# Five routed blocks moved between the heads of the matrix memory, one bank for its query products, result gathers behind all masks

## What is computed

```python
# cross attention (per sequence, 8 heads of 16 features)
log_D = log_fg_mat + ig[:, None, :]
max_log_D = jnp.max(log_D, axis=-1, keepdims=True)
D_mat = jnp.exp(log_D - max_log_D)
qk = jnp.einsum('hsd,htd->hst', qh, kh) / np.sqrt(DH)
C = qk * D_mat
normalizer = jnp.maximum(jnp.abs(C.sum(axis=-1, keepdims=True)), jnp.exp(-max_log_D))
h = jnp.einsum('hst,htd->hsd', C / (normalizer + EPS), vh)

# mixture of experts: 8 experts, 128 -> 512 -> 128, two per token
h = jax.nn.gelu(jnp.einsum('bsd,edi->bsei', x, ew1) + eb1)
all_outputs = jnp.einsum('bsei,eid->bsed', h, ew2) + eb2
moe_out = jnp.einsum('bse,bsed->bsd', weights_E, all_outputs)
return x + _mlp(x, sh_w1, sh_b1, sh_w2, sh_b2) + moe_out
```

## Time and profile before

| | |
|---|---|
| median of 3 runs | 2514.45 us (2510.74 to 2525.26) |
| the profiled execution | 2516.93 us |
| its span, first to last instruction | 2514.5 us |
| mean granted clock of TensorE | 0.896 of full |
| busy: PE, DVE, ACT, POOL | 1936.6, 1697.9, 1113.0, 842.5 us |

### The profile page before, as it was taken

One profiled execution on the slowest core, in us unless ns is written; L12 is line 12 of the kernel. 1 busy time (PEld: TensorE's weight loads), 2 busy tenths in 40 slices (PEclk: granted clock), 3 DMA queues, 4 the chain that ended last, 5 costly groups with the idle time before them and its releaser, 6 DMA issues.

```text
span 2514.5 us, 41889 instructions
## 1 busy us (share of the span) xinstructions
PE 1936.6 (77%) x14136; PEld 1372.4 (55%) x14136; DVE 1697.9 (68%) x3985; ACT 1113.0 (44%) x3168; POOL 842.5 (34%) x775
## 2 busy tenths in 40 slices
PE   2785697778886898678876788679876888675698
PEld 1454366645673457545674467445664567454355
DVE  8985893679656893769556993769556883723355
ACT  2462365335642465236542565236632565232234
POOL 0551562217420651227321651236321651211000
PEclk8997899889997999889987999789987999787799
DMA  4000012101030013101030103001120103042000
GB/s 134 1 1 9 15 54 71 63 10 60 5 121 11 22 47 99 35 11 59 18 107 11 52 17 110 24 13 58 39 86 11 66 2 113 13 169 90 9 13 21
DMA packets 72770, 117.33 MB, mean 47 GB/s; under 512 B 7823, under 2 KB 46871, under 8 KB 72039
## 3 DMA queue, kind: packets, MB, share of 16 engines
q1 hardware_dynamic: 67014, 101.42, 12.3%
q0 software_dynamic: 5536, 13.12, 1.7%
HBM read 95.18 MB, written 18.81 MB: 45 GB/s over the span
## 4 chain that ended last, share of the span: by engine, by line
DVE 37%; PE 36%; issue 14%; POOL 6%; ACT 5%; DMA 1%; SPq 1%; DVEq 0%; POOLq 0%; ACTq 0%
PE bank L1336 34%; DVE work L495 11%; DVE bank L504 5%; DVE work L513 3%; DVE work L493 3%; DVE max L782 2%; ACT work L941 2%; POOL hid L1244 1%; PE bank L1340 1%; DVE acc L698 1%; POOL work L1212 1%; POOL work L1224 1%; ACT hid L941 1%; PE bank L1481 1%; DVE negmax L515 1%
## 5 line engine op out<-in xcount | busy, mean ns | idle before, releaser
L1336 PEld LDWEIGHTS bank<-work 128*128 128x128 f32 (+2 forms) x5152 | 372.3, 187 | 171.1 <-issue 143.8
L1336 PE MATMUL bank<-work 128*128 128x128 f32 (+2 forms) x5152 | 403.0, 293 | 55.7 <-DVE max L782 29.2
L941 ACT ACTIVATE work<-bank 128x512 f32<-128x512 f32 (+1 forms) x560 | 246.5, 518 | 283.6 <-PE bank L1336 257.5
L495 DVE TENSOR_TENSOR work<-bank,table_space 64x512 f32<-64x512 f32 x512 | 352.1, 688 | 6.8
L1212 POOL TENSOR_TENSOR work<-work 128x512 f32<-128x512 f32 x128 | 163.3, 1276 | 385.7 <-DVE work L495 284.6
L941 ACT ACTIVATE work<-work 128x512 f32<-128x512 f32 (+1 forms) x338 | 196.7, 618 | 170.1 <-DVE work L576 84.8
L941 ACT ACTIVATE work<-work,negmax 128x128 f32<-128x128 f32 x512 | 199.1, 390 | 100.3 <-DVE negmax L515 100.3
L1219 POOL TENSOR_TENSOR work<-sb_ident,nrm 128x512 f32<-128x512 f32 x128 | 133.0, 1039 | 284.2 <-ACT nrm L941 284.2
L1336 PE MATMUL bank<-work,table_space 128*128 128x512 f32 x256 | 140.5, 630 | 90.0 <-DVE negmax L515 59.5
L941 ACT ACTIVATE hid<-bank,w_ring 128x128 f32<-128x128 f32 x480 | 136.1, 370 | 163.6 <-PE bank L1336 163.5
L493 DVE TENSOR_TENSOR work<-bank,table_space 128x512 f32<-128x512 f32 x256 | 174.0, 679 | 48.7 <-PE bank L1336 22.6
(11 more groups left out here) (287 smaller groups left out, 3478.6 us busy)
## 6 DMA issues: line engine op xcount, KB each, us to landing
w_ring<-in_w_routed SPq DMA_DIRECT2D x120, 514.0 KB, 4.3
x_quad<-x_sorted SPq DMA_DIRECT2D x24, 256.0 KB, 2.8
y_sorted<-y_quad SPq DMA_DIRECT2D x24, 256.0 KB, 2.5
x_T<-in_x_T POOLq DMA_DIRECT2D x9, 256.0 KB, 3.1
x_row<-in_x_row POOLq DMA_DIRECT2D x9, 256.0 KB, 4.5
ctx_T<-in_ctx_T SPq DMA_DIRECT2D x8, 256.0 KB, 2.7
work<-in_ctx_row SPq DMA_DIRECT2D x8, 256.0 KB, 2.9
out<-act_row SPq DMA_DIRECT2D x8, 256.0 KB, 2.3
```

What stands on the lines that cost most here:

```text
L495: last = v.tensor_tensor(rows(wk[i + 1][o]), rows(src[p]), sinT[o, s].unsqueeze(1).broadcast_to([DH0, GB, N]), ALU.mult)
L941: return nc.scalar.activation(o, i, f, **k)
L1336: return nc.tensor.matmul(o, l, r, start=start, stop=stop, skip_group_check=True)
```

## The change

Five edits, all between the end of the gate computation and the combination:

1. With heads beside them, units 12 to 16 (blocks 10 to 14) and the down product of block 9 are no longer computed ahead of `xattn` but between its heads, by two tables on PE (`UP_AT`, `DOWN_AT`), one on ACT (`GELU_AT`) and places in DVE's loop.
2. All query products go through bank 7, so the product of head s waits for the mix of head s - 1, and it stands behind the value product of head s - 2. Maxima alternate between banks 0 and 5, value products are in banks 1 and 2.
3. The masked contexts have four tiles of their own, so POOL no longer waits for the transposed rows ahead of masks 2 and 3.
4. POOL makes all 8 masks first; then it waits for the stores, then computes the context mean (`cbc`, before on DVE in `attn1`), then gathers 8 times in a row.
5. The transposes of the last routed rows stand at unit 10 instead of unit 12.

The pieces of the diff are, in this order: the tables; `xattn` of VectorE; `xattn` of ScalarE; `rows_back` and `xattn` of GpSimd; `xattn` of TensorE.

```diff
+        head_ctx, decay1, mix1 = wk[16:20], wk[14:16], wk[12:14]
+        nv_bank, max_bank = (1, 2), (0, 5)
...
+        BEFORE_X = 12
+        UP_AT, DOWN_AT = {0: 12, 1: 13, 3: 14, 4: 15, 5: 16}, {0: 11, 3: 12, 4: 13, 5: 14, 6: 15, 8: 16}
+        GELU_AT = {1: (12, 13), 3: (14, 15), 5: (16,)}
...
@@ -573,21 +579,25 @@
                         last.then_inc(arg_done, 1)
+                    if d and 4 <= s < 8:
+                        take_block(s + 6, g)
                     h = s - 1
                     if h >= 0:
...
+                    if d and s == 0:
+                        take_block(9, g)
+                if d:
+                    take_block(14, g)
                 dve.wait_ge(num, n1(H1))
...
@@ -1045,13 +1053,17 @@
+                gates_total(g, d)
                 for h in range(H1):
                     act.wait_ge(arg_done, tally(g, d, H1, h + 1))
+                    fn(decay1[h % 2], decay1[h % 2], ACT.Exp).then_inc(dmat, 1)
+                    if d and h in GELU_AT:
+                        for j in GELU_AT[h]:
+                            gelus(j, g, j == GELU_AT[h][-1])
...
@@ -1238,6 +1248,10 @@
                 for s in range(2):
                     pool.wait_ge(y_stored[s], g * (LOAD // 2 * 16) + LOAD // 2 * 16)
+                q.tensor_tensor(cbc[:], csum[:].unsqueeze(2).broadcast_to([128, GB, N]),
+                                per_token.unsqueeze(2).broadcast_to([128, GB, N]), ALU.mult).then_inc(ctx_mean, 1)
+                for i in range(TOPK * GB):
+                    gather(g, i)
@@ -1249,18 +1263,13 @@
-                    if d and 2 <= h < 4:
-                        pool.wait_ge(quad_tr, g * LOAD + h + 1)
-                    if d and h == 4:
-                        rows_back(g)
                     if h >= 4:
                         pool.wait_ge(qk1, tally(g, d, H1, h - 3))
...
-                    if d and 4 <= h:
-                        gather(g, 2 * h - 8)
-                        gather(g, 2 * h - 7)
+                if d:
+                    rows_back(g)
@@ -1593,38 +1601,46 @@
-                        mm(bank[4 + s % 2][:], sel24[:, s], m_parts[:]).then_inc(mx_bc, 1)
-                        pe.wait_ge(ctx_masked, n1(s + 1))
-                        if s == 0 and d:
-                            pe.wait_ge(y_out, g * BLOCKS + BLOCKS)
-                        if s >= 2:
-                            pe.wait_ge(c_done, n1(s - 1))
...
+                        mm(bank[max_bank[s % 2]][:], sel24[:, s], m_parts[:]).then_inc(mx_bc, 1)
+                    if d and s in DOWN_AT:
+                        experts_down(DOWN_AT[s], g, d, True)
+                    if d and s in UP_AT:
+                        experts_up(UP_AT[s], g, d, True)
                     h = s - 2
                     if h >= 0:
                         pe.wait_ge(c_done, n1(h + 1))
...
+                    if s < H1:
+                        pe.wait_ge(ctx_masked, n1(s + 1))
+                        if s == 0:
+                            pe.wait_ge(gate_eM, tally(g, d, 1, 1))
+                        else:
+                            pe.wait_ge(c_done, n1(s))
+                        for b in range(GB):
+                            last = mm(rows(bank[7])[:, b], rows(head_ctx[s % 4])[:, b], rows(seq_T)[:, b],
+                                      start=b == 0)
+                        last.then_inc(qk1, 1)
```

More of the change, by code:

```diff
@@ L91, in decoder @@
         rank = cols[:, 32:40]
+        per_token = cols[:, 20:20 + GB]
         block_no = cols[0:1, 72:72 + BLOCKS]
@@ L133, in decoder @@
         y_back = [hid[2], hid[3]]
-        head_ctx = [wk[2], wk[3]] + [x[:].rearrange("p b d -> p (b d)") for x in x_quad]
+        head_ctx, decay1, mix1 = wk[16:20], wk[14:16], wk[12:14]
+        nv_bank, max_bank = (1, 2), (0, 5)
         class Norm:
@@ L575, in xattn @@
                         for b in range(GB):
-                            last = v.scalar_tensor_tensor(rows(wk[s % 2])[:, b], rows(bank[4 + s % 2])[:, b],
+                            last = v.scalar_tensor_tensor(rows(decay1[s % 2])[:, b], rows(bank[max_bank[s % 2]])[:, b],
                                                           aT[:, b, s:s + 1], mask_ji[:], ALU.add, ALU.add)
                         last.then_inc(arg_done, 1)
+                    if d and 4 <= s < 8:
+                        take_block(s + 6, g)
                     h = s - 1
@@ L746, in heads_and_experts @@
                     take_block(7, g)
+                    take_rows(3, g)
                     take_block(8, g)
-                    take_block(9, g)
-                    take_rows(3, g)
-                    for i in range(10, BLOCKS):
-                        take_block(i, g)
+                    if not heads:
+                        for i in range(9, BLOCKS):
+                            take_block(i, g)
             def experts_norm(g):
@@ L1097, in heads_and_experts @@
                 if experts:
-                    for j in range(7, UNITS):
-                        gelus(j, g, j == UNITS - 1)
-                if heads:
-                    gates_total(g, d)
+                    for j in range(7, BEFORE_X if heads else UNITS):
+                        gelus(j, g, j in (BEFORE_X - 1 if heads else UNITS - 1,))
             def router_exp(g, d):
@@ L1319, in _ @@
             rows_back(G - 1)
-            for i in range(TOPK * GB):
-                gather(G - 1, i)
             attn1(G - 1)
@@ L1507, in unit @@
                         experts_down(j - 1, g, d, heads)
-                    if experts and j in (0, 4, 8, 12):
-                        rows_T(j // 4, g, d, heads)
+                    if experts and j in (0, 4, 8, 10):
+                        rows_T((j + 2) // 4, g, d, heads)
                 for s in range(H0 + 7):
@@ L1560, in heads_and_experts @@
                     gate_tot_columns(g, d)
-                for j in range(12, UNITS + 1):
-                    unit(j)
+                else:
+                    for j in range(BEFORE_X, UNITS + 1):
+                        unit(j)
             gw = res["gate_w"]
@@ L1595, in gate_tot_columns @@
                 pe.wait_ge(gate_tot, tally(g, d, 1, 1))
-                gate_columns(bank[0], gate[3], gate_T)
+                gate_columns(bank[7], gate[3], gate_T)
             def xattn(g, d):
                 n1 = lambda k: tally(g, d, H1, k)
-                nv = [bank[2 + i][:, 0:2 * H1 * (DH1 + 1)].rearrange("p (b h d) -> p b h d", b=2, h=H1)
-                      for i in range(2)]
+                nv = [bank[i][:, 0:2 * H1 * (DH1 + 1)].rearrange("p (b h d) -> p b h d", b=2, h=H1) for i in nv_bank]
                 for s in range(H1 + 2):
@@ L1608, in xattn @@
                             pe.wait_ge(gate_max, tally(g, d, 1, 1))
-                        mm(bank[4 + s % 2][:], sel24[:, s], m_parts[:]).then_inc(mx_bc, 1)
-                        pe.wait_ge(ctx_masked, n1(s + 1))
-                        if s == 0 and d:
-                            pe.wait_ge(y_out, g * BLOCKS + BLOCKS)
-                        if s >= 2:
-                            pe.wait_ge(c_done, n1(s - 1))
-                        for b in range(GB):
-                            last = mm(rows(bank[6 + s % 2])[:, b], rows(head_ctx[s % 4])[:, b], rows(seq_T)[:, b],
-                                      start=b == 0)
-                        last.then_inc(qk1, 1)
+                        if s == 1 and d:
+                            pe.wait_ge(quad_T, g * LOAD + LOAD)
+                        mm(bank[max_bank[s % 2]][:], sel24[:, s], m_parts[:]).then_inc(mx_bc, 1)
[3 more added lines that the diff above has]
+                        experts_up(UP_AT[s], g, d, True)
                     h = s - 2
@@ L1874, in layouts @@
     cols[:, 32:40] = 8 - np.arange(8)
+    cols[:, 20:20 + GB] = 1 / N
     cols[:, 72:] = np.arange(BLOCKS)
```

16 lines of the change are left out of this document (7 added, 9 removed).

## The result

The changed kernel takes **2624.73 us** (median of 4 runs, 2612.95 to 2628.7), the kernel before in the same job 2512.59. The ratio is **1.0434 [1.0403, 1.0466]**: 4.3% slower, 112 us. I had forecast 2585 (+70.5), in a range from 2558 to 2622: the measured time lies 2.7 above its end. The profiled execution takes 2623.85, its span is 2622.1, and TensorE's mean granted clock is 0.878 (before 0.896). Busy are PE 1989.7, DVE 1674.1, ACT 1166.9 and POOL 850.8 us. In the lines, argument, mix, copy, denominators and combination of DVE are now L582, L593, L700, L602 and L708; PE's products are L1343.

The account below looks back on a forecast made before the run. PE was taken to bound both merged stretches. Seven turns +60.9, group 0 +8.4 and last group +1.2 give +70.5 on the profiled 2516.93: 2587.4; that execution lies 2.5 above the median, so 2585 us, range 2558 to 2622 (80%).

Parts of the forecast that it names:

- The sign and the mechanism: Slower, 94%: in xattn, one bank makes a 3.18 us loop per head, copies behind the argument 5.40 in heads 4 and 5.
- both terms: Per turn: gate columns to denominators +5.2 us, denominators to combination +4.5.
- my sum: Whole kernel: seven turns +60.9, first group +8.4, last group +1.2, together +70.5 us.
- that rival: Merged stretch: TensorE falls to half clock; with half the heads there, some 8 us a turn, 2640 us; 9%.
- Group 0: Eight heads without blocks, half clock in the first two loops: +8.4 us; 6 if the clock rises at once, 15 if never.
- This is the largest term, and gathers set it, not PE: Behind the last copy: store wait, mean and 8 gathers start the combination at 1335.6, 9.7 us later than before.
- my rival: DVE's norms beside the gathers hold them up, at most 5 us: 2600 to 2620; 12%, shared with ACT's thin covers failing.
- ACT's loads: Three added pairs of table loads, 7.7 us a turn, costed at nothing because covered, by 0.2 and 0.1 us at the thinnest.
- the mean taken off DVE: In attn1, DVE loses the context mean; it waited there for PE's products anyway, so nothing gained.
- the combination shortened: Combination beside POOL's residual sums: 3.4 us instead of 4.40, so -1.0 a turn, bounds 0 and -2.1.
- "Unchanged": Behind the combination, attn1 was to stay unchanged; combination to the next gate columns was forecast at 0.

Follow-up runs that it names:

- PE kept busy: The changed kernel with products that nobody reads added where PE waits, no wait shortened: 2578.84 us, ratio 1.0249.
- the version in pairs: The kernel before with its gathers later but in pairs, a mask or half of the context mean on POOL between two pairs: 2504.94 us, ratio 0.995.

## Why the prediction was right, and where it was short

- **The sign and the mechanism were right.** One bank closes the loop at 3.26 a head, and the copy behind the argument makes it 5.54. Undoing the one saves 42 us, the other 55; both together leave 0.4% of the 4.3%. The size was short: +112 against +70.5. That the time came as near to the range as 2.7 is in part luck: the rest of the turns gave back 18.3 that no term of mine had.
- **The step that failed is the clock.** I costed every product of the merged stretch at its duration at full clock, and gave its fall 9%. It fell in all seven turns (0.75 to 0.87 against 1.00). That is 13.6 a turn where I had 5.2. With the waits filled the clock stays up and both terms are those of my sum, which shows the cause for the turns. I argued against the fall from `attn1`, where PE was busy 5.27 of 12.70 at 0.90; a nearer row was the earlier trace rows, where the query product of group 0 took 1.91 already. The Trainium skill (page "TensorE: Matmul & The Clock Gate", section "HAM oscillation — how this bites in real kernels") describes a loop whose waits let the clock fall on every pass. The rows here agree in part: the waits were 1.0 to 1.5 us, shorter than that loop's, and the clock fell behind some of them only (it held at 1.00 for 15.8 us in the turn shown). My price for that rival, 2640 with half the heads at half clock, was near.
- **Group 0 was the same mistake.** I let the clock rise after two loops (+8.4, "15 if it stays at half"). It stayed at 0.50: +17.1.
- **"This is the largest term, and gathers set it, not PE" was half right.** The gathers do end last (DVE waits 4.56 for a DMA). But they start behind PE's last blocks, and most of the delay is PE's: the denominators came 13.6 later, the gathers added 2.9 beyond the norms. At full clock, with PE kept busy, it was 5.8 and 4.5, near my 5.2 and 4.5.
- **The norms hold up the gathers a little.** In the turn shown, the gathers beside the norm's two products on DVE took 1.06 and 1.40 instead of 0.96; in the other six turns one took 1.06 to 1.08. The Trainium skill (page "SBUF — State Buffer", section "SBUF: two separate sides") names such a lock; here it would be worth 0.5 us in one turn and 0.1 in the others, against the 15 to 35 us in all of my rival.
- **ACT's loads and the mean taken off DVE changed nothing**, as costed; the combination shortened by 1.3 (forecast 1.0). The mean ahead of the gathers does cost: with three quarters of it ahead of the wait for the stores the combination started 13.3 to 13.5 behind the denominators, and not 13.4 to 14.2.
- **"Unchanged" for the rest of the turn was wrong**: it was 18.3 shorter over six turns. The granted clock goes with it. In the kernel before the rest takes 232.4 to 238.7 from turn to turn; these are two of its turns, then one of the changed kernel:

```profile
1047.43:1286.12 238.69, 193.75 (x1447) 132.87 (x1447) 167.10 (x370) 116.59 (x349) 89.27 (x80) 0.91 0.14 44
1330.36:1563.10 232.74, 187.62 (x1446) 129.68 (x1446) 167.12 (x369) 116.35 (x349) 89.34 (x80) 0.94 0.14 45
1688.33:1921.48 233.15, 187.90 (x1449) 129.96 (x1449) 165.99 (x369) 117.34 (x350) 90.29 (x81) 0.94 0.14 45
```

The work is the same, PE's time is 6 us longer where the clock is lower, and so is the turn. The clock is 0.91 in two of the six turns before, 0.93 in three and 0.94 in one; in the changed kernel it is 0.93 in one and 0.94 in five. At 0.94 the rest takes 232.7 before and 230.0 to 233.3 in the changed kernel; that the mean taken off DVE in `attn1` shortens it is not shown. What sets the clock there no run here isolates. Most of the 0.5% that the version in pairs gains lies there too: its combination starts only 0.4 earlier in a turn, and its rest takes 232.5 to 232.9 in four of six turns.

## What to carry to other kernels

Before work is put into an engine's gaps, ask what it waits for there: a product placed behind a wait, or a copy queued behind another operation on the reader's engine, turns the gap into a longer loop. If the engine is TensorE, price every product of a stretch with new waits at both clocks, and take as evidence a loop of the same shape in the same trace. And what follows the filled stretch decides whether filling pays: here the best filling saved 2.5 us a turn and gave it back to gathers that could start only behind it.

## What was not expected of the hardware

- Added products that nobody reads made the kernel 46 us faster, since the granted clock stayed at full (1.00 against 0.75 to 0.87).
- In group 0 the clock stayed at 0.50 with two banks in the new order although PE was busy 32.75 of 32.80 us, and rose with the old order (21.4 us at 0.81). So PE's recorded busy time alone does not tell whether the clock rises. Which difference lets it rise is open.
- A row of eight gathers issued by POOL held PE's products beside it up: the denominators came 5.1 to 6.7 us later a turn, the fall of the clock behind it included; in pairs with 0.6 to 1.05 us of other POOL work between them the same gathers held up nothing. That PE's products end late is read from their semaphores and from the reader, since the ends of products in the profile are modelled. The Trainium skill (page "SBUF — State Buffer", section "SBUF: two separate sides") says that PE waits for no other engine there; whether the hold-up lies in that memory or elsewhere these runs do not show.
